# Half-length scans of a MetaFormer kernel: VectorE multiplies two following states by C in one instruction where their PSUM banks adjoin, and GpSimd's states are chosen anew for each lane

## The reference, cut to what matters

```python
def step(h, inp):                       # h: channels x 16 states
    dtt, ut, bt, ct = inp
    dA = jnp.exp(dtt[..., None] * A)    # "decay", 16 states
    h = h * dA + (dtt * ut)[..., None] * bt[:, :, None, :]   # "drive"
    y = jnp.einsum('bkdn,bkn->bkd', h, ct)                   # weigh by C, add over the states
    return (h, y)
```

## Time and profile before

| | |
|---|---|
| median of 3 runs | 5605.96 us (5604.6 to 5613.72) |
| the profiled execution | 5607.85 us, span 5606.0 us |
| VectorE busy | 4445.6 us, 79% of the span |
| GpSimd busy | 3960.4 us, 71% |
| ScalarE busy | 3634.0 us, 65% |
| TensorE busy | 4828.6 us, 86% (its spans overlap, so this is not TensorE at its peak) |
| lanes of layer 0, three images | about 30 us each |
| lanes of layer 1, three images | about 30.4 us each |

### The profile page before, as it was taken

The page is one execution under the profiler, slowest core; times in us unless marked ns, Lnnn a source line. Parts: engine busy times, 40 slices in busy tenths (PEclk is TensorE's granted clock), DMA queues, the critical chain, the costliest instruction groups (busy, mean ns, idle before and its releaser), DMA issues. The chain is left out here.

```text
span 5606.0 us, 73119 instructions
## 1 busy us (share of the span) xinstructions
PE 4828.6 (86%) x23205; PEld 3411.3 (61%) x23205; DVE 4445.6 (79%) x4529; ACT 3634.0 (65%) x5725; POOL 3960.4 (71%) x3074
## 2 busy tenths in 40 slices
PE   7888797789898887888989888888998988888998
PEld 5776546656666645555666645565666654556777
DVE  6889838959999848977999957996999975896544
ACT  5666455448887757767878857775878865775222
POOL 5888619839999818857999935894999962984111
PEclk9999999989999998998999999998999999999999
DMA  5777607737877616647788724654877842562110
GB/s 206 263 252 264 211 10 258 252 132 254 287 268 268 226 34 219 224 135 250 260 280 271 269 69 171 220 183 161 281 266 276 271 166 102 201 216 93 43 43 29
DMA packets 356676, 1104.83 MB, mean 197 GB/s; under 512 B 33210, under 2 KB 121126, under 8 KB 354872
## 3 DMA queue, kind: packets, MB, share of 16 engines
q1 hardware_dynamic: 356280, 1100.06, 56.9%
HBM read 1086.24 MB, written 13.68 MB: 196 GB/s over the span
## 5 line engine op out<-in xcount | busy, mean ns | idle before, releaser
L1157 PE MATMUL banks<-ident,prod 128*128 128x128 f32 x4752 | 764.9, 287 | 392.5 <-DVE prod L1458 286.6
L1157 PEld LDWEIGHTS banks<-ident,prod 128*128 128x128 f32 x4752 | 556.8, 145 | 799.1 <-DVE prod L1458 557.8
L1449 DVE TENSOR_TENSOR_SCAN banks<-banks,h 128x512 f32<-128x512 f32 x594 | 723.3, 1218 | 85.8 <-ACT banks L1297 48.5
L1400 POOL TENSOR_TENSOR h<-lane,Bb 128x512 f32<-128x512 f32 x576 | 722.8, 1272 | 57.8 <-DMA Bb<-half_rows 33.8
L1297 ACT ACTIVATE banks<-lane,A 128x512 f32<-128x512 f32 x864 | 581.1, 686 | 251.6 <-DVE prod L1458 82.4
L1229 PE MATMUL banks<-w_a,Cb 128*128 128x384 f32 x1536 | 552.2, 488 | 0.0
L1449 DVE TENSOR_TENSOR_SCAN banks<-banks,half_carry_a,h 128x512 f32<-128x512 f32 x396 | 505.5, 1277 | 8.8 <-ACT banks L1297 4.9
L1400 POOL TENSOR_TENSOR h<-half_du_a,Bb 128x512 f32<-128x512 f32 x384 | 482.7, 1275 | 14.8 <-DMA Bb<-half_rows 10.1
L1297 ACT ACTIVATE banks<-half_delta_a,A 128x512 f32<-128x512 f32 x576 | 385.3, 685 | 151.5 <-DVE lane L1430 73.7
L1217 PE MATMUL banks<-big,w_a 128*128 128x256 f32 x1728 | 435.0, 394 | 1.0 <-DMA w_a<-w_in 0.8
L1458 DVE TENSOR_TENSOR prod<-banks,half_C_a 128x512 f32<-128x512 f32 x528 | 365.3, 692 | 73.4 <-DMA half_C_a<-half_rows 2.4
(11 more groups left out here) (471 smaller groups left out, 12291.6 us busy)
## 6 DMA issues: line engine op xcount, KB each, us to landing
Bb<-half_rows SPq DMA_DIRECT2D x576, 512.0 KB, 4.3
C_first<-rows SPq DMA_DIRECT2D x288, 512.0 KB, 5.4
Cb<-half_rows SPq DMA_DIRECT2D x288, 512.0 KB, 4.4
w_a<-w_in SPq DMA_DIRECT2D x256, 576.0 KB, 6.1
w_b<-w_in SPq DMA_DIRECT2D x128, 576.0 KB, 6.2
half_C_a<-half_rows SPq DMA_DIRECT2D x128, 512.0 KB, 6.7
Bb<-rows SPq DMA_DIRECT2D x96, 512.0 KB, 5.5
half_C_b<-half_rows SPq DMA_DIRECT2D x64, 512.0 KB, 6.6
```

The source lines that it names most:

```text
L1157: mm = eng.matmul(ps[:, 0, at], src[:, at], m.ident[:, :], start=n == 0 and k == 0, stop=added(s) == (i + 1) * N, is_transpose=True, skip_ ...
L1400: eng.tensor_tensor(m.dBu[:, s % DRIVES, :], m.du[i % 2], m.B[b % BRING][:, cols(s % 2)], ALU.mult).then_inc(st.dbu, 1)
L1449: eng.tensor_tensor_scan(flip(to), flip(slot(s)), flip(m.dBu[:, s % DRIVES, :]), initial, ALU.mult, ALU.add).then_inc(st.scanned, 1)
```

## The change

`units_of` joins two following states of a lane into a unit when VectorE weighs both and their banks adjoin (the ring's places follow each other and don't wrap). A unit of two is weighed by one instruction of 128x1024 behind the second scan, and its last values are kept by one copy of 128x2. For each lane, `split` picks the five GpSimd states, with gaps of 2 to 4, so that the units are fewest; most often it takes n = 2, 4, 7, 10, 13. Worked out from the rules, layer 0 has 103 pairs in the 24 lanes of an image (161 units where there were 264 weighings) and layer 1 has 48 in its 12 lanes (84 units for 132), so 453 pairs over the three images. States 5 and 6 are a pair in 19 of the 24 lanes and in 7 of the 12. The three product buffers become twice as wide, `turned_sum` moves, and two inputs of layer 1 (`late_input`) move to make room.

```diff
+    POOLED, GAPS = 5, (2, 3, 4)
...
-    def by_pool(s):
-        return s % N % 3 == 1
...
+    def neighbours(s):
+
+        return place_of["step", s + 1] == place_of["step", s] + 1 and place_of["step", s] % SLOTS < SLOTS - 1
+
+    def units_of(i, theirs):
+
+        units, n = [], 0
+        while n < N:
+            two = n + 1 < N and n not in theirs and n + 1 not in theirs and neighbours(i * N + n)
+            if n not in theirs:
+                units.append((i * N + n, i * N + n + 1) if two else (i * N + n,))
+            n += 1 + two
+        return units
+
+    def pool_choices(chosen):
+        if len(chosen) == POOLED:
+            return [chosen] if N - 3 - chosen[-1] < GAPS[-1] else []
+        begin = [chosen[-1] + gap for gap in GAPS] if chosen else GAPS
+        return [c for n in begin if n < N - 2 for c in pool_choices(chosen + (n,))]
+
+    def split(i):
+
+        return min(pool_choices(()), key=lambda c: (len(units_of(i, c)), sum((y - x - 3) ** 2 for x, y in zip(c, c[1:])), c))
+
+    theirs_in = [split(i) for i in range(LANES)]
+
+    def by_pool(s):
+        return s % N in theirs_in[s // N]
...
         else:
-            eng.wait_ge(st.prod, own(b) + 1)
+            eng.wait_ge(st.prod, unit_index[b] + 1)
             if first_half(b):
-                eng.wait_ge(st.kept, kept(b + 1)[0])
+                eng.wait_ge(st.kept, keep_index[b])
...
-            def keep(s):
-                eng.wait_ge(st.prod, own(s) + 1)
-                eng.activation(carry(s), last_state(s, slot(s)), ACT.Copy).then_inc(st.kept, 1)
+            def keep(u):
+                eng.wait_ge(st.prod, unit_index[u[0]] + 1)
+                eng.activation(carry(u[0], len(u)), last_states(u), ACT.Copy).then_inc(st.kept, 1)
...
-            def weigh(s):
-                n = s % N
-                eng.wait_ge(st.c[n // 2], 16 * (group(s) + 1))
-                if own(s) >= PRODS:
-                    eng.wait_ge(st.summed, added(own_steps[own(s) - PRODS]))
-                eng.wait_ge(st.scanned, s + 1)
-                eng.tensor_tensor(prods[own(s) % PRODS], slot(s), m.C[:, n, :], ALU.mult).then_inc(st.prod, 1)
+            def weigh(u):
+                k, n = unit_index[u[0]], u[0] % N
+                for pair in sorted({s % N // 2 for s in u}):
+                    eng.wait_ge(st.c[pair], 16 * (group(u[0]) + 1))
+                if k >= PRODS:
+                    eng.wait_ge(st.summed, added(units[k - PRODS][0]))
+                eng.wait_ge(st.scanned, u[-1] + 1)
+                eng.tensor_tensor(prods[k % PRODS][:, 0:len(u), :], slots(u), m.C[:, n:n + len(u), :],
+                                  ALU.mult).then_inc(st.prod, 1)
...
                 if s < STEPS:
                     scan(s)
-                    if not by_pool(s):
-                        weigh(s)
+                    if s in ends_unit:
+                        weigh(ends_unit[s])
```

More of the change, by code:

```diff
@@ L924, in fused_scans @@
     held = [m.held[:, b, :] for b in range(HELD)]
-    prods = [m.prods[:, b, :] for b in range(PRODS)]
+    prods = m.prods
     def pair_at(v, part):
@@ L978, in fused_scans, with slots @@
+    def slots(u):
+        first = 1 + place_of["step", u[0]] % SLOTS
+        return ps[:, first:first + len(u), :]
     keeps = {}
[L979 to L982, removed]
+    for u in keep_order:
+        until = place_of["step", u[0]] + SLOTS
+        keeps.setdefault(max(s for s in range(u[0], u[0] + SLOTS + 1) if place_of["step", s] <= until), []).append(u)
@@ L1142, in dt_product, with add @@
                            stop=True).then_inc(st.dt, 1)
[L1144 to L1148, removed]
-                else:
-                    src = prods[own(s) % PRODS]
-                    eng.wait_ge(st.prod, own(s) + 1)
-                if n == 0 and i:
-                    eng.wait_ge(st.copied, i)
[L1155 to L1158, removed]
+            def add(a):
+                i = a[0] // N
+                if by_pool(a[0]):
+                    src = [held[pooled(a[0]) % HELD]]
+                    eng.wait_ge(st.pooled, pooled(a[0]) + 1)
+                else:
+                    k = unit_index[a[0]]
+                    src = [prods[k % PRODS][:, r, :] for r in range(len(a))]
+                    eng.wait_ge(st.prod, k + 1)
+                first, last = a == first_add[i], a == last_add[i]
+                if first and i:
+                    eng.wait_ge(st.copied, i)
+                for r in range(len(a)):
+                    for k in range(HALF // P):
+                        at = slice(k * P, (k + 1) * P)
+                        mm = eng.matmul(ps[:, 0, at], src[r][:, at], m.ident[:, :], start=first and r == 0 and k == 0,
+                                        stop=last and r == len(a) - 1, is_transpose=True, skip_group_check=True)
                 mm.then_inc(st.summed, 1)
@@ L1345, in _ @@
                 i, n = s // N, s % N
-                for b in keeps.get(s, ()):
-                    keep(b)
+                for u in keeps.get(s, ()):
+                    keep(u)
                 if s < STEPS:
@@ L1831, in acc @@
     def acc(f, c):
[L1832 removed]
+        return late_input(m, f) if c and f in LATE_SILUS else m.prod[:, f % 3, cols(c)]
     def out_bank(r):
```

84 lines of the change are left out of this document (48 added, 36 removed).

## The result

The changed kernel takes **5696.65 us** (median of four runs, 5693.86 to 5697.78) against 5605.59 for the kernel before in the same series: ratio 1.0156, 95% interval 1.014 to 1.0172. It is 91 us slower. The forecast had 34 us slower, with 5692 us as its upper end.

What follows compares the result with a forecast made beforehand. VectorE was taken to bound second halves, GpSimd first halves, ScalarE some 0.25 us behind. Layer 0 at +11 us per image, +33 for three, layer 1 and the rest 0, gave 5640 us (+0.6%), range 5585 to 5692.

Steps and rivals of the forecast that it cites:

- The mechanism that the prediction walked: Lanes pairing states 5 and 6: later weighing delays decay 8, block and decay 9; scan 9 waits 2.1 us.
- The saving on VectorE: VectorE's queue: each pair saves about 0.29 us, 131 us over 453 pairs, the most that can come back.
- The rule of the Trainium skill: Semaphores between VectorE instructions cost nothing extra, so a pair saves only 0.06 us; as a rival 5715 us, chance 0.03.
- Lanes without the pair 5, 6: -0.7: GpSimd has state 5, decay 8 is early, VectorE keeps about 0.29 x 4; five layer 0 lanes, -3.5 us.
- second half, no evictions, with 5, 6: Layer 0: the new wait at scan 9 costs +0.8 us a lane; six lanes, +5.5 us per image.
- first half, no evictions: Layer 0: GpSimd sets scan 0, late pairs give nothing; +1.5 us a lane, four lanes +5.6 per image.
- first half, evictions: Layer 0: 30.95 against 29.94 us, +1.0 a lane; five lanes, +5.0 us per image.
- TensorE's adds: 0: Same number of adds, later and in bursts of eight, hidden by VectorE; uncovered, `down` holds the second GELU up to 0.4 us.
- fall into the new wait: Layer 0 second halves: evictions at n = 8 are absorbed ahead of scan 9; -0.45 us a lane, four lanes -1.6.
- Layer 1 "0": Layer 1: 7 lanes with states 5 and 6 paired at about +0.5 us against 5 at -0.7, sum 0.
- deeper waits: Rival: blocks at n = 2 and n = 13 also late, 0.5 us more in 108 lanes; 5694 us, chance 0.17.
- the saving is kept: Rival: second halves keep 4.2 pairs of 0.29 us each, -66 us, first halves at GpSimd's pace; 5540 us, chance 0.2.

Runs made afterwards that it cites:

- run 1: The changed kernel with each pair weighed by two narrow instructions behind its second scan; 5698.87 us.
- run 2: The changed kernel with states 5 and 6 weighed singly, all other pairs kept; 5640.03 us.
- run 4: The changed kernel with Identity for the experts' GELU, and so without the blocks' table loads; 5539.66 us.
- run 6: The changed kernel with layer 0's GELU block behind decay 8 moved behind decay 9; 5645.39 us.
- run 9: Against the kernel before: pairs and new GpSimd states only where VectorE sets the pace, block behind decay 9 in lanes pairing 5 and 6; 5593.85 us.
- run 3: The changed kernel with no pairs, every state weighed singly, GpSimd's new states kept; 5621.14 us.
- run 5: The kernel before the change with Identity for the experts' GELU, without the blocks' table loads; 5553.98 us.
- run 11: The changed kernel in layer 0 only, layer 1's lanes as before the change; 5665.29 us.
- run 12: The changed kernel with TensorE's delta product of the next lane ahead of a lane's first add; 5675.61 us.
- run 7: The kernel before the change with layer 0's block behind decay 8 moved behind decay 9; 5617.98 us.
- run 8: The kernel of run 6 with layer 0's block behind decay 2 also moved behind decay 3; 5715.0 us.

## Why the prediction was wrong

**The mechanism that the prediction walked held, in the lanes that it walked.** The held banks delay decay 8, the block delays decay 9, scan 9 waits. By the walk 9.42 us from scan 5 to scan 9, measured 9.32; lane 15 at 30.2, measured 30.5. Runs 1, 2, 4, 6 and 9 all bear it out: the wait shrinks to under a third when the pair is split, it goes when the block is gone and when the block is moved, and it stays when only the wide instruction is taken away. The saving on VectorE was right too: 1.19, 1.42 and a weighing of 1.225 long (range up to 1.384), 1.14 to the next. The rule of the Trainium skill that a semaphore costs nothing extra ("VectorE: DVE Perf Modes", section "The DRAIN you can't avoid") was measured there on eight copies in a row. This trace does not agree with it for a scan and what follows: the wide weighing starts 1.42 us after its scan, the delta that needs nothing of it 1.18.

**The step that failed: "Lanes without the pair 5, 6: -0.7".** The prediction counted them as pure gain (GpSimd has state 5, decay 8 is early) and never walked them. Layer 0 has five of them and layer 1 five, -3.5 each per image. In layer 0 the four that can be compared are at -0.1, -0.8 and -0.2 us together in the three images; in layer 1 the five are at +4.8, +7.0 and +6.7. That is 36 of the 57 us that lie between the +33 forecast and the +90 of the profiled executions, 29 of them in layer 1. Second halves of layer 0 are 15 us above their terms, first halves 4, what lies outside the lanes 13; the rest, mostly layer 1's lanes with the pair and its last lane, is 11 below.

**The other terms.** Layer 0 was put at +11 per image, measured +20. For the first image, lane by lane, last lane left out:

| kind of lane | predicted | measured |
|---|---|---|
| second half, no evictions, with 5, 6 (6 lanes) | +5.5 | +10.1 |
| second half, evictions (4) | -1.6 | -0.1 |
| first half, no evictions (4) | +5.6 | +5.8 |
| first half, evictions (5) | +5.0 | +4.9 |
| no pair 5, 6 (5 predicted, 4 here) | -3.5 | -0.1 |

In the other two images the second halves without evictions are at +8.0 each. That the first halves agree is partly luck: lanes 0, 1, 7 and 13 are at -0.2, +1.3, +1.4 and +3.2 where +1.5 each had been said, and those with evictions lie between +0.1 and +1.7 around +1.0.

- *Lanes without the pair 5, 6, layer 0*: I took four savings of 0.29 for granted and walked only the lanes with the new wait. Lane 19 waits 2.2 us for decay 14 and 0.5 for decay 9, lane 12 waits 1.3 for GpSimd at state 15; only lanes 6 and 17 gain, 0.6 and 0.3. Lane 19 is +0.8 in run 3 already: its new GpSimd states cost it that, not its pairs.
- *Second halves at +0.8 or +0.9 each*: lane 15 is at +1.1, but lanes 3 and 11 have the delta wait on top (1.3 and 1.1 us), through TensorE's queue. "TensorE's adds: 0" was wrong for a reason that the sum never held: not the number of adds but what is queued behind one that waits.
- *Evictions "fall into the new wait"*: so they do at n = 9 (0.3 to 1.2 left of 2.0), but lanes 10, 14, 16 and 18 then wait 0.4, 0.7, 0.7 and 1.9 us at the eviction for `down` (the expert's second product), and 10 and 16 another 0.6 each for decay 14.
- *Layer 1 "0"* was +4.3, +7.4 and +6.2. The six lanes with the pair that can be compared are +1.8 to +2.3 together (+0.5 each said), and the last lane gives about 2 us back. The rest is in lanes without the pair: 2 and 5 at +1.3 each, 9 at +3.7, and in two images lane 0 at +1.
- *Small slips of the working*: 9.53 + 13.1 + 7.85 + 0.4 is 30.9 and not 30.95; six times +0.8 is 4.8 and not 5.5, four times +1.5 is 6.0 and not 5.6. None moves the forecast by more than 3 us.
- *VectorE's busy time* fell by 52 us where 72 had been named.

In lanes 2 and 5 of layer 1 the pair is 6 and 7, and the `keep` of that pair stands in ScalarE's queue ahead of decay 8. So "decay 8 is early" does not hold there. Lane 2, ScalarE and then VectorE, after:

```profile
2212.77 0.17 ACT L1338 ACTIVATE half_carry_a<-banks 128x2 f32<-128x2 f32 x1 [2.92 <-DVE half_more_a L1508]
2212.84 0.69 ACT L1346 ACTIVATE banks<-lane,A 128x512 f32<-128x512 f32 x1
...
2217.71 1.23 DVE L1498 TENSOR_TENSOR_SCAN banks<-banks,h 128x512 f32<-128x512 f32 x1 [2.93 <-ACT banks L1346]
```

The keep waits 2.92 us for the wide weighing (1.18 for the narrow one before), decay 8 and the block follow it, and scan 9 waits 2.93 us where it waited 1.90. It is the prediction's own mechanism, by another pair and by a keep instead of a bank. The block is not all of it: without the loads (run 4 against run 5) scan 9 does not wait, and the two lanes are still 1.0 us longer, with 0.8 of waiting for GpSimd at state 8.

Lane 9 of layer 1 in the changed kernel, all engines in order of time:

```profile
2432.68 4.45 PE L1217 MATMUL banks<-big,w_out_a 128*128 128x512 f32 x6 [3.44 <-DVE prod L1508]
...
2438.27 2.74 PE L1217 MATMUL banks<-big,w_out_a 128*128 128x512 f32 x6
...
2441.05 0.60 ACT L1350 ACTIVATE big<-banks 128x512 f32<-128x512 f32 x1 [5.94 <-PE banks L1217]
...
2442.40 1.29 DVE L1498 TENSOR_TENSOR_SCAN banks<-banks,half_carry_a,h 128x512 f32<-128x512 f32 x1 [4.30 <-ACT banks L1346]
```

The output product (L1217) waits for its bank, which a later weighing now releases; `copy_out` (L1350) stands in ScalarE's queue ahead of decay 12 and waits 5.94 us for that product; scan 12 waits 4.30. In the kernel before the same copy waited 1.02 us. In this lane too the pair is 6 and 7, and the bank is that of state 6. It is not the table loads: without them (run 4) the copy waits 6.01. No run splits the pair 6, 7 by itself, but the runs narrow it down. With the new GpSimd states and no pairs (run 3) lanes 2, 5 and 9 are 0.3, 0.2 and 0.2 us longer than before the change. With the pairs weighed by two narrow instructions (run 1) they are 1.5, 1.4 and 4.0 longer, and with only 5 and 6 apart (run 2) 1.3, 1.3 and 3.7. So it is the held-back weighing of a pair other than 5, 6, and run 11 gives the whole of layer 1 back.

**Which case came.** The time is that of the rival "deeper waits" (5694), but only partly its mechanism, so that the number fits is in part luck: 9.1 us of waits per image at state 14 (4.4 before) and 3.5 at state 3 (none before), and `down` late at evictions. It had put 0.5 us into every lane; what came was 1 to 3 us in some lanes and nothing in others. The rival "the saving is kept" did not come; run 4 against run 5 shows that even with the block gone the layer 0 lanes keep only 35 of 89 us.

**Open.** In the profiled executions 12.6 us lie outside the changed lanes. The granted TensorE clock is lower there: 0.91 against 0.93 in a stretch ahead of the lanes, and 0.81 against 0.87 in the gap behind layer 1. But the other kernels' traces have the same code there, and in them the stretch ahead of the lanes takes 1225.7 to 1240.3 us and the gap 70.1 to 76.9, with the pairs (run 1: gap 70.1, clock 0.92) as well as without them (run 3: gap 74.2). So these 12.6 us are not shown to be the change's. All four runs of the change lie within 4 us of each other, but no run here shows why unchanged code has another clock. Of what runs 11 and 12 gain in their profiled executions, 17 and 11 us lie in such stretches and not in the lanes.

## What to carry to other kernels

When an instruction is delayed to join another, walk what it releases: here a decay that started 1.1 us later, for a bank freed later, stood ahead of a block of 3.4 us on an in-order queue. Do that walk in every kind of lane and through every queue, TensorE's adds and ScalarE's copies too, before booking a gain for the lanes that seem free: those were the terms that failed. In this kernel it paid to make the change only where the relieved engine sets the pace, and to move the block with it: that turned +91 us into -13.

## What the runs showed that I had not expected

- A move of one block by one step was worth -51 us (run 6 against the change), +9 us (run 7 against the kernel before) and, with a second block moved too, +70 us (run 8 against run 6).
- Without the 576 table loads of the blocks the changed kernel is 157 us faster and the kernel before 55 us, though ScalarE's busy time fell by about 750 us in each (3593.6 to 2830.6, 3634.0 to 2891.6).
- Two narrow weighings back to back take 1.29 us and one wide takes 1.23: the 453 saved instructions alone are worth 2 us of the time, no more than the runs scatter.
